# Four engine orders and a DMA queue of a two-layer attention and feed-forward kernel written out anew, with four weight loads side by side

## What is computed

```python
x = x + L0_xattn(_layernorm(x), ctx)   # energy = (ctx Wq^T + bq)(ctx Wk^T + bk)^T; x_m = LN(x) softmax(energy)^T
x = x + L0_ffn(_layernorm(x))          # RMS norm * w_norm; 8-bit rows; ternary weights; value * silu(gate); ternary out
x = x + L1_xattn(_layernorm(x), ctx, mask)   # 16 heads, 8 key/value heads of 128; softmax; Wo
x = x + L1_ffn(_layernorm(x))          # fp8-rounded gate, up (256 x 768) and down (768 x 256), three scales
```

## Time and profile before

| | us |
|---|---|
| median of 3 runs | 313.87 |
| lowest and highest of them | 310.63, 313.88 |
| profiled execution, its own time | 312.58 |
| its span, first to last instruction | 310.5 |

### The profile page before, as it was taken

How to read it: one execution, slowest core, us unless ns; L and a number is a source line. 1 busy time by engine, 2 the same in 40 slices (tenths; PEclk the granted TensorE clock), 3 DMA queues, 4 the chain that set the end, 5 groups by cost and what they waited for, 6 DMA issues and landing times.

```text
span 310.5 us, 6396 instructions
## 1 busy us (share of the span) xinstructions
PE 293.6 (95%) x1980; PEld 259.9 (84%) x1992; DVE 260.9 (84%) x713; ACT 253.7 (82%) x603; POOL 218.5 (70%) x290
## 2 busy tenths in 40 slices
PE   3968999999999999999999999999999999999994
PEld 2755487798989998979889999999988999899884
DVE  3959999999999999889999986997768897675665
ACT  2398995598999998979999899778899999855460
POOL 3558864556998578999879998886678798952001
PEclk9979999999999999999999999999999999999999
DMA  7996032001326548885878756537645647200103
GB/s 223 367 381 199 35 101 70 1 8 30 93 47 189 157 138 251 220 212 139 228 210 226 199 144 174 161 108 219 182 144 148 179 143 211 68 3 0 36 1 101
DMA packets 54609, 44.59 MB, mean 144 GB/s; under 512 B 11696, under 2 KB 45104, under 8 KB 54576
## 3 DMA queue, kind: packets, MB, share of 16 engines
q1 hardware_dynamic: 54016, 43.93, 49.0%
q10 hardware_dynamic: 560, 0.26, 0.3%
HBM read 27.01 MB, written 15.20 MB: 136 GB/s over the span
## 4 chain that ended last, share of the span: by engine, by line
PE 59%; DVE 20%; DMA 8%; issue 5%; SPq 4%; ACT 2%; DVEq 0%
PE pb L2016 41%; DMA block_room<-blocks 5%; PE pb L2279 5%; PE pb L2314 4%; DMA wraw<-in_wgvT 3%; DVE blocks L1581 3%; SPq L442 2%; DVE sm L1564 2%; PE pb L2130 2%; PE pb L2091 2%; PE pb L2076 2%; DVE wraw L1455 2%; DVE step L1601 1%; PE pb L2227 1%; DVE q_lo L1551 1%
## 5 line engine op out<-in xcount | busy, mean ns | idle before, releaser
L667 POOL TENSOR_TENSOR tp_lo<-tp,pT_hi 128x512 fp32r<-128x512 f32 x54 | 70.0, 1311 | 15.1 <-ACT pT_hi L993 14.8
L981 ACT ACTIVATE sm<-sm,smin 128x256 f32<-128x256 f32 x128 | 63.6, 501 | 4.7 <-DVE smin L1564 4.4
L1564 DVE CUSTOM_DVE_ANT_0 sm<-pb,mask_all 128x256 f32<-128x256 f32 x128 | 47.3, 418 | 5.6 <-PE pb L2016 5.5
L1581 DVE STREAM_TRANSPOSE blocks<-sm 128x1024 f32<-128x1024 f32 x27 | 33.5, 1240 | 7.4 <-DMA block_room<-blocks 7.0
L2016 PE MATMUL pb<-ctx_hi,q_hi 128*128 128x256 f32 x128 | 38.1, 298 | 1.1 <-DVE q_lo L1551 0.6
L662 POOL TENSOR_SCALAR sm<-sm,srec 128x256 f32<-128x256 f32 x64 | 30.5, 488 | 10.4 <-DVE srec L1570 10.4
L2016 PE MATMUL pb<-xT_hi,m_hi 128*128 128x256 f32 x128 | 37.3, 292 | 0.3 <-DVE xT_lo L1540 0.3
L2016 PE MATMUL pb<-n_hi,oT_hi 128*128 128x256 f32 x128 | 37.1, 290 | 0.2 <-DVE oT_lo L1595 0.2
L2016 PE MATMUL pb<-xT_hi,m_lo 128*128 128x256 f32 x128 | 36.2, 283 | 0.0
L2016 PE MATMUL pb<-xT_lo,m_hi 128*128 128x256 f32 x128 | 36.2, 283 | 0.0
L2016 PE MATMUL pb<-ctx_lo,q_hi 128*128 128x256 f32 x128 | 36.2, 282 | 0.0
(11 more groups left out here) (195 smaller groups left out, 943.0 us busy)
## 6 DMA issues: line engine op xcount, KB each, us to landing
block_room<-blocks SPq DMA_DIRECT2D x108, 128.0 KB, 2.8
tp<-block_room SPq DMA_DIRECT2D x54, 256.0 KB, 3.0
w_raw<-in_w SPq DMA_DIRECT2D x4, 576.0 KB, 4.6
wraw<-in_wgvT SPq DMA_DIRECT2D x4, 512.0 KB, 8.4
wraw<-in_woutT SPq DMA_DIRECT2D x2, 512.0 KB, 9.3
out<-xb SPq DMA_DIRECT2D x4, 256.0 KB, 2.2
xa<-in_x SPq DMA_DIRECT2D x3, 256.0 KB, 4.5
xb<-in_ctxT SPq DMA_DIRECT2D x2, 256.0 KB, 5.1
```

The costliest lines, as they stand in the source:

```text
L667: g.tensor_tensor(tp_lo[:, z, c, :], tp[:, z, c, :], as_f32(pT_hi[:, c, :]), ALU.subtract).then_inc(pT_lo_pool, 1)
L981: a.activation(sm[:, n % 2, k, :], sm[:, n % 2, k, :], ACT.Exp, bias=smin[:, n % 2, k:k + 1], scale=-1.0, accum_out=ssum[:, n % 2, k:k + 1 ...
L1564: v.tensor_tensor_reduce(out=sm[:, n % 2, k, :], in0=bank(passing_bank("s", 2 * n + h))[:, (k % 2) * S:(k % 2 + 1) * S], in1=mask_all[:, b ...
L1581: v.transpose(blocks[:].rearrange("p g k b -> p k g b"), sm[:, n % 2, :, :].rearrange("p k (g b) -> p k g b", b=32)).then_inc(blocks_done, 1)
```

## The change

The body of no function is changed. What changes is the order of the calls in all five lists, the bank of nearly every entry of `PASSING`, and the banks of the sums that stay (`SUMS` from 7 to 2, `DOWN` from ((5, 6), (2, 7)) to ((6, 4), (1, 2))). The same instructions are issued, as many on each engine. On SP, the loads of the quarters 1, 2 and 3 move from behind the block writes 7 and 12 to ahead of block write 3, and `eighth(0)` from behind `turn_rows(2)` to ahead of it; `scales` moves from the first loads to behind block write 10; `contexts(1)` moves up by three loads and `hidden_out(0)` down by two.

SP's list:

```diff
             rows(1)
+            contexts(1)
             rows(2)
             rows(3)
             gate_value(0)
-            contexts(1)
             gate_value(2)
-            hidden_out(0)
             gate_value(1)
             gate_value(3)
+            hidden_out(0)
             hidden_out(1)
             raw(0)
             raw(4)
             raw(5)
-            norm_weight()
             raw(6)
             raw(1)
+            norm_weight()
             raw(3)
-            scales()
             raw(8)
             raw(2)
-            turn_rows(1)
             raw(9)
             mask_bytes()
+            turn_rows(1)
             raw(7)
+            eighth(0)
             turn_rows(2)
-            eighth(0)
             turn_hidden(2)
             turn_hidden(3)
+            eighth(1)
+            eighth(2)
+            turn_rows(3)
+            eighth(3)
             blocks_written(3)
-            turn_rows(3)
             blocks_read(3)
             blocks_written(4)
             blocks_read(4)
             blocks_written(5)
+            blocks_written(6)
             blocks_read(5)
-            blocks_written(6)
             blocks_read(6)
             blocks_written(7)
-            eighth(1)
             blocks_read(7)
...
             blocks_written(10)
+            scales()
+            blocks_read(10)
             blocks_written(11)
-            blocks_read(10)
+            blocks_written(12)
             blocks_read(11)
-            blocks_written(12)
-            eighth(2)
-            eighth(3)
             blocks_read(12)
```

The start of TensorE's list, and the place of the last fused products:

```diff
             rows1(1)
+            project1(2)
             energy(1)
+            project1(3)
             turn_context(0)
-            project1(2)
-            project1(3)
             probs(0)
             weight_sum(0)
-            mix(0)
             energy(2)
             turn_kv(0)
             turn_kv(1)
+            mix(0)
             probs(1)
             energy(3)
-            rows1(2)
+            weight_sum(1)
             turn_kv(2)
             turn_kv(3)
-            weight_sum(1)
...
             queries(2)
-            fuse_vo(7)
+            scores(1, 0)
             turn_queries(7)
-            scores(1, 0)
             scores(1, 1)
-            queries(3)
             fuse_qk(5)
+            fuse_qk(6)
+            fuse_qk(7)
             probs4(0, 0)
             probs4(0, 1)
-            fuse_qk(6)
+            fuse_vo(7)
+            queries(3)
             scores(2, 0)
             scores(2, 1)
-            fuse_qk(7)
             contexts(0, 0)
+            contexts(0, 1)
             value_half(3, 1)
-            contexts(0, 1)
             probs4(1, 0)
             probs4(1, 1)
+            gate_half(4, 0)
```

VectorE's list around the first ternary weights:

```diff
             weight_mean(0)
             sums(2)
+            maxima1(2)
+            inverse1(1)
             ternary(0)
+            ternary(1)
+            ternary(2)
             added1(0)
             weight_sums(1)
             second_stats(0)
+            ternary(3)
             centred(0)
+            weight_mean(1)
             maxima1(3)
             scaled(0)
```

More of the change, by code:

```diff
@@ L1747, in _ @@
             masked(4, 0)
+            outputs_low(1)
             q_low(5)
@@ L1813, in _ @@
             eighths(5)
-            q_low(13)
+            inverse(11)
             inverse(12)
+            outputs_low(7)
+            q_low(14)
+            second(4)
             turn_blocks(11)
-            second(4)
-            second(5)
+            outputs_low(8)
             masked(13, 0)
             masked(13, 1)
+            second(5)
             third_stats(2)
+            added3(0)
+            turn_blocks(12)
             inverse(13)
-            outputs_low(8)
-            added3(0)
-            q_low(14)
-            turn_blocks(12)
             masked(14, 0)
@@ L1879, in _ @@
             masked(20, 0)
+            outputs_low(15)
             masked(20, 1)
-            turn_blocks(19)
-            outputs_low(15)
+            inverse(19)
+            second(6)
             second(7)
-            masked(21, 0)
             inverse(20)
             third_stats(3)
+            turn_blocks(19)
+            eighths(9)
+            masked(21, 0)
+            q_low(22)
             masked(21, 1)
-            q_low(22)
+            outputs_low(16)
+            added3(1)
             turn_blocks(20)
-            added3(1)
@@ L1989, in _ @@
             fused(6)
+            output(0, 1)
+            fuse_low(6)
             fused(7)
-            fuse_low(6)
+            fused(8)
             fuse_low(7)
-            fused(8)
+            fuse_low(8)
             fused(9)
-            fuse_low(8)
             fused(10)
@@ L2444, in _ @@
             scores(7, 1)
+            value_half(5, 0)
             queries(8)
+            queries(9)
             contexts(3, 0)
             contexts(3, 1)
-            queries(9)
             scores(8, 0)
             scores(8, 1)
+            queries(10)
+            value_half(5, 1)
             contexts(4, 0)
-            queries(10)
+            queries(11)
             contexts(4, 1)
-            queries(11)
+            scores(9, 0)
+            scores(9, 1)
+            queries(12)
+            contexts(5, 0)
@@ L2455, in _ @@
             attn_out(3, 0)
-            value_half(5, 1)
-            scores(9, 0)
-            gate_half(6, 0)
-            scores(9, 1)
-            contexts(5, 0)
-            attn_out(3, 1)
             contexts(5, 1)
-            queries(12)
             scores(10, 0)
             scores(10, 1)
-            value_half(6, 0)
+            queries(13)
+            attn_out(3, 1)
             attn_out(4, 0)
+            attn_out(4, 1)
             contexts(6, 0)
             contexts(6, 1)
-            attn_out(4, 1)
@@ L2471, in _ @@
-            queries(13)
+            gate_half(6, 0)
             scores(11, 0)
             scores(11, 1)
+            gate_half(6, 1)
             attn_out(5, 0)
-            attn_out(5, 1)
+            ffn_out(4)
             contexts(7, 0)
             contexts(7, 1)
-            gate_half(6, 1)
+            attn_out(5, 1)
             scores(12, 0)
             scores(12, 1)
+            queries(14)
+            gate_half(7, 0)
             attn_out(6, 0)
-            attn_out(6, 1)
-            ffn_out(4)
@@ L2484, in _ @@
-            ffn_out(5)
+            scores(13, 0)
+            scores(13, 1)
             contexts(8, 0)
             contexts(8, 1)
+            attn_out(6, 1)
+            value_half(6, 0)
             attn_out(7, 0)
+            ffn_out(5)
+            gate_half(7, 1)
+            value_half(6, 1)
+            value_half(7, 0)
             attn_out(7, 1)
-            scores(13, 0)
-            scores(13, 1)
-            gate_half(7, 0)
-            queries(14)
             contexts(9, 0)
             contexts(9, 1)
-            queries(15)
@@ L2511, in _ @@
             contexts(11, 1)
+            queries(17)
             scores(16, 0)
-            attn_out(9, 0)
+            scores(16, 1)
             attn_out(9, 1)
-            scores(16, 1)
             attn_out(10, 0)
```

894 lines of the change are left out of this document (439 added, 455 removed), and 52 rows, old and new, of the table PASSING.

## The result

The change makes the kernel slower. Its median is 317.56 us over 4 runs (315.93 to 317.88), that of the kernel before, run beside it, 313.36 (310.63 to 313.88): a ratio of 1.0142 with a 95% interval from 1.009 to 1.0194. The changed kernel run once more among the experiments gave 1.0167 (1.0133 to 1.0201). The forecast was 312.5 with a range up to 316.4. The profiled execution has a span of 315.4 us against 310.5. A few executions (two of e3's twelve among them) fell in a slower state of the chip; the ratios leave them out, so a ratio can differ a little from that of two medians.

The account below looks back on a forecast made before the run. The prediction took TensorE, nearly always busy, as the bound, so only waits could move. Its terms, -0.8 - 0.5 + 0.3 + 0.0 - 0.4 = -1.4 us, moved the median from 313.87 to 312.5 us, range 308.7 to 316.4.

Parts of the forecast that it names:

- What bounds the kernel: Whole kernel: TensorE busy 293.6 of 310.5 us; only waits can move, at most 9.7 us to win, little behind 160 us.
- Part 1: First loads and first 40 us: hidden_out(0) earlier brings layer 0's last weights 1.4 us sooner, mix(0) later; -0.8 us taken.
- Part 2: Quarter loads: -0.5 us for leaving their old places, +0.3 us for standing ahead of block write 3.
- the loads ahead of write 3: Three quarter loads delay block write 3, landing near 97 us; bounds 0 and +1.7 us, taken +0.3.
- step 3's products are far down TensorE's list: At block write 3: the reason given for taking only +0.3 us within bounds of 0 and +1.7.
- the old places: Around block writes 7 and 12: two places lose the quarter loads as neighbour; gain 0 to 1.5 us, taken -0.5.
- Part 3: Five orders between 40 and 300 us: at most 5.1 us to win, 4 to lose; middle taken, rounded to -0.4.
- the bound of +4: Orders between 40 and 300 us: the most they could lose, +4 us, taken from the slower rival.
- The slower rival: 60 to 160 us: VectorE's rounding meets GpSimd at new places, durations don't carry over; +4 to +5.5 us, 318; chance 0.14.
- point of decision: 60 to 160 us: the slower rival decides once VectorE's extra time exceeds its slack of 6.6 us.
- Nothing reaches the end: Whole kernel: each local gain is eaten by the next wait; median stays at 313.9 within 0.5 us; chance 0.19.

Follow-up runs that it names:

- e3: All five lists in the new order up to probs4(1, 1), near 80 us, old behind it, quarters 1 to 3 at old places; 314.43 us, ratio 1.0083.
- e2: Kernel before with only the quarter loads moved: 0 ahead of turn_rows(2), 1 to 3 ahead of block write 3; 313.69 us, ratio 1.0084.
- e7: Kernel before with quarter loads 1 to 3 right behind turn_hidden(2), where the DMA engines are idle; 312.26 us, ratio 0.997.
- after_again: The changed kernel word for word, run once more; 318.49 us, ratio 1.0167 to the kernel before.
- e1: Changed kernel with all four quarter loads back at their old places, new orders kept; 318.33 us, ratio 1.0241 to the kernel before.
- e9: Changed kernel with quarter loads 1 to 3 directly behind turn_hidden(2); 318.09 us, ratio 1.0214 to the kernel before.
- e6: Changed kernel with GpSimd's outputs_split(0), (1) and (2) moved earlier; 315.03 us, ratio 1.0088 to the kernel before.
- e4: Old orders up to probs4(1, 1), new ones behind it, quarters 1 to 3 at the new place; 314.37 us, ratio 1.0095 to the kernel before.
- e8: Changed kernel with ScalarE's context_high(0) again ahead of projected1(0); 315.99 us, ratio 1.0151 to the kernel before.
- e10: Changed kernel with the edits of e6, e8 and e9 together; 312.89 us, ratio 1.0046 to the kernel before.
- e11: As e10, with the edit of e5 too; 312.05 us, ratio 1.0028 to the kernel before.
- e5: Changed kernel with VectorE's probs_low(0, 0), probs_low(0, 1) and inverse(1) ahead of scaled(3); 317.26 us, ratio 1.0106 to the kernel before.

## Why the prediction was wrong

**What bounds the kernel.** Right in its frame: the matmuls' time did not change, and only waits moved. Wrong in its use: "a moderately bad one costs little" was said of the time behind 160 us, where TensorE was idle for 0.4 of 140 us. All kernels with the new lists behind 80 us take 35.8 to 37.2 us from queries(18) to attn_out(16,0) for the old 34.55, 1.2 to 2.6 more (of those with the old lists e2 and e3 have 34.86 and 34.26, but e7 36.13), although VectorE has 26 us to spare in the stretch. Slack as a sum over 140 us did not protect a single due time.

**Part 1, -0.8 us.** The number is near (-0.97 at queries(2) in the profiled execution, but -0.06 in after_again), and that is luck: gate_half(0, 0) starts at 33.43 us for 33.49, so 0.91 of the 0.97 arose behind the stage that Part 1 reckons with. The steps are half right. ScalarE's second sum did come earlier, from 14.51 us (estimate 14.9, 16.31), and mix(0) started at 19.76 (estimate 20.1). But the spreading matmul came at 17.17 instead of 16.3, as VectorE's list has wpart behind other work; the table load of 1.28 us was not thought of at all (a call at the head of a list was taken as free to move); and the gate products begin when they did, as L1498 of scaled(0) came at 30.55 us ( 30.25). TensorE's waits for pr (2.8 us) and gbuf (1.4) stand in between and probably ate the lead; no run moved them. What moves the start most, the moment at which TensorE's rate rises, stood in no step.

**Part 2, -0.5 and +0.3.** The signs were right and both sizes wrong. The +0.3 for the loads ahead of write 3 (bounds 0 to 1.7) measured +2.5 in the old orders (e2, outside the bounds) and +0.87 in the new. In the changed kernel the write landed at 100.32 us, not near 97:

```profile
96.10 4.22 DMA block_room<-blocks
```

Two things add there. Its last part took 4.22 us instead of 2.8, and SP issued it from 94.66 instead of 91.81, as VectorE's transpose ahead of it ended only at 94.65: the first loss is passed on. e2 has the loads' share alone: issued from 92.03, landed at 98.95. The movement of three quarters was reckoned from the issue of the first, but it was the last of them, issued at 93.17, that stood in front of the write, and the step "step 3's products are far down TensorE's list" looked at the wrong user: the waiting instruction is VectorE's next transpose, and all of VectorE's list stands behind it. The -0.5 for the old places (0 to -1.5) measured -2.1 in the new orders (e1 against the changed kernel, stage to queries(18)), -1.0 in the old ones (e2), and +0.3 in e7. In sum the quarters' move is worth -1.2 us over both stages in the new orders, better than the -0.2 forecast, and costs 1.5 in the old ones. VectorE's waits for the block writes, of which the forecast expected less, grew from 7.0 us to 11.4 in all; but e7, as fast as the kernel before, has 12.2, so their sum does not tell the loss.

**Part 3, -0.4.** This is the step that failed. It took the middle between two bounds for want of rows that spoke for either order (the middle of -5.1 and +4 is -0.55, a slip that decides nothing), and so set the price of the new collisions off against gains that no row promised. It measured, with the quarters taken out (e1), +5.46 us behind queries(2), beyond even the bound of +4. Two of its pieces are named above: +1.84 from VectorE meeting GpSimd at 66 to 76 us, and 2.08 between queries(18) and attn_out(16,0), which may in part be scatter, as e7 has 1.58 there with the old lists. A third, +0.75, is what e1 and e9 still have in the second stage, and e1 has 1.5 more by queries(18) with its wait for tp_lo. On top of this comes the granted clock, 1.6 us in half of the executions, which the prediction set aside.

**The slower rival** (0.14, 318 us) came nearest to the time, and its mechanism, durations that don't carry over to another neighbour, is what e6 shows. Its place was wrong, so that its time came out near is luck: not the rounding L1601, whose median went from 489 to 624 ns and which nobody waited for, but `centred` and `scaled(3)`. So was its point of decision: VectorE's busy time in 60 to 160 us fell to 91.33 and never came near 97. 1.7 us more in ten suffice, as TensorE's list asks for pT_lo at one moment; total slack says nothing there. The Trainium skill ("SBUF — State Buffer", Who interferes with whom) calls the port pair that VectorE and GpSimd share an exclusive lock. The rows agree: an instruction on 128 x 2 numbers ends within 0.05 us of GpSimd's, at 74.75 and 75.78.

**Nothing reaches the end** (0.19) is refuted for losses. For gains it has something: e9's local gain of 0.85 us does not show in its median. But e7 against e2, and e6 against after_again, show local gains of 2.5 and 2.6 us that reach the end.

**What stays open.** Which calls cost 1.2 to 2.6 us between 167 and 207 us, and how far it is the orders at all, as e7 has 1.58 of it with the old ones. The trace names waits of 0.9 us for a transposed hidden tile (uqT), 0.3 for oT_lo and 0.25 for xn, which make 1.4, but no experiment moved them alone. Nor was it tried what makes the clock fall after the same wait in one execution and not in another. The start has the like: behind the wait at L2166 the granted clock over 15 to 20 us is 0.80 in the kernel before (wait 2.40 us) and 0.84 in e2 (1.33), but 1.00 in e4 (1.45).

## What to carry to other kernels

A plan laid out with one run's durations holds the collisions of that run in it, and a planner that gives each instruction one duration will put an expensive pair together elsewhere; plan with a price for the pair, and look at the small instructions right ahead of what TensorE needs next. Before a load is put ahead of a transfer in the same queue, ask what waits for that transfer and what is queued behind the waiter. And compare stages between places with the same work ahead of them, not spans: they repeated to 0.3 us where a median of 12 runs has an interval of 0.6%.

## What the runs showed that was not expected

**The start of TensorE.** In all 14 profiled executions TensorE's first matmuls go out about 0.44 us apart (in e8 eight in 3.54 us) and the same kind 0.215 apart later (four in 0.86), a factor of two, so 1.2 and 2.4 GHz, while the granted clock in the records says 1.00 for both. The Trainium skill ("TensorE: Matmul & The Clock Gate", Part 1) says that an idle array starts at 1.2 GHz; the spacing agrees, the record of the granted clock does not show it. The moment of the rise varies. Where ScalarE's context_high(0) stood first and the first matmuls followed each other without a gap (before, e2, e4, e7, e8, e10, e11), full rate was reached by 12.5 us every time. Where the table load left a gap of 0.57 to 0.93 us behind them, it was reached by the first energy in three executions (after, e1, e3; in after and e3 already within the first eight matmuls, ahead of the gap), and only behind 13.5 us in four (after_again, e5, e6, e9). From the first matmul to L2166 the three took 11.0 us and the four 12.8 to 13.2. That the gap is the cause fits most of these numbers and was not tested by itself; if so, the new first call costs about 2 us in half of the executions beside its 0.8.

**A table load has a place.** It takes 1.28 us in both traces of e8's section, and it sits in front of whichever activation comes first, L886 or L870. It cost the path nothing at 2.23 us, where the context was still on its way. The Trainium skill ("ScalarE: Activation LUTs", What ACT_TABLE_LOAD costs) states about 1283 ns for the load itself; the traces agree.

**One wait of 1.8 us can cost 3.4**, by the clock behind it: e6 shortened the wait by 0.7 us, and the stage by 2.6.
